# Six of twelve shifts of a grouped convolution as plain fp32 products on 32- and 64-column tiles, and the first mixing in fp32

## The reference

```
x = x + L0(x); x = x + L1(x); x = x + L2(x); x = x + L3(x)

L0, L2:  att   = softmax(mlp(cond) @ W2 + b2)            # (128 samples, 8)
         agg_w = einsum('bk,koi->boi', att, weight)      # a 128 x 128 matrix for each sample
         out   = einsum('boi,bih->boh', agg_w, x) + (att @ bias_k)[:, :, None]
L1, L3:  out   = conv1d(x, weight, 9 taps, padding 4, 4 groups of 32 channels)
                 + (cond @ c_weight.T)[:, :, None] + bias[None, :, None]
```

## Time and profile before

| | |
|---|---|
| median of 3 runs | 2906.19 us (2905.75 to 2907.77) |
| profiled execution: its own time, its span | 2907.99 us, 2905.7 us |
| PE, PEld busy | 2882.7 us (99%), 2860.9 us (98%) |
| DVE, ACT, POOL busy | 2420.1 us (83%), 1668.6 us (57%), 1482.6 us (51%) |
| instructions of PE | 49240 matmuls, as many loads |
| granted clock, mean over the span | 0.997 |

### The profile page before, as it was taken

How to read it: one execution, slowest core, us unless ns; L and a number is a source line. 1 busy time by engine, 2 the same in 40 slices (tenths; PEclk the granted TensorE clock), 3 DMA queues, 4 the chain that set the end, 5 groups by cost and what they waited for, 6 DMA issues and landing times.

```text
span 2905.7 us, 122950 instructions
## 1 busy us (share of the span) xinstructions
PE 2882.7 (99%) x49240; PEld 2860.9 (98%) x49240; DVE 2420.1 (83%) x2589; ACT 1668.6 (57%) x2593; POOL 1482.6 (51%) x1546
## 2 busy tenths in 40 slices
PE   8999999999999999999999999999999999999998
PEld 7999999999999999999999999999999999999998
DVE  8888888888888888888888888888888888888884
ACT  5555555555555555556565656565556555655564
POOL 3445554555455545544554455445544554455452
PEclk9999999999999999999999999999999999999999
DMA  6777777777777777777777777777777777777774
GB/s 160 198 199 201 202 196 203 198 202 196 202 197 202 198 202 196 204 196 204 193 204 197 204 193 206 198 203 194 204 199 203 197 200 200 202 203 193 201 202 138
DMA packets 374536, 573.17 MB, mean 197 GB/s; under 512 B 63336, under 2 KB 226800, under 8 KB 358128
## 3 DMA queue, kind: packets, MB, share of 16 engines
q1 hardware_dynamic: 325744, 506.17, 63.8%
q10 hardware_dynamic: 48768, 66.65, 9.1%
HBM read 271.63 MB, written 167.77 MB: 151 GB/s over the span
## 4 chain that ended last, share of the span: by engine, by line
PE 98%; DVE 1%; ACT 0%; DMA 0%; issue 0%; ACTq 0%; SPq 0%
PE ps L354 74%; PE ps L339 24%; ACT x_t L530 0%; DVE prod L592 0%; DVE y L635 0%; DVE m_sum L595 0%; PE ps L267 0%; PE ps L262 0%; DMA mixed<-m_own 0%; DVE m_own L603 0%; DMA m_parts<-mixed 0%; DVE m_own L601 0%; DVE xp L627 0%; DVE conv_parts L567 0%; ACT L449 0%
## 5 line engine op out<-in xcount | busy, mean ns | idle before, releaser
L354 PE MATMUL ps<-y,conv_parts 32*128 32x512 f32 x36864 | 2735.2, 390 | 2.2 <-DVE y L635 2.2
L354 PEld LDWEIGHTS ps<-y,conv_parts 32*128 32x128 f32 x36864 | 2533.4, 184 | 17.5 <-issue 2.3
L500 ACT ACTIVATE y<-ps,bias 128x512 fp32r<-128x512 f32 x1536 | 1045.4, 690 | 748.6 <-PE ps L354 710.6
L635 DVE SCALAR_TENSOR_TENSOR y<-ps,bias,y 128x512 fp32r<-128x512 f32 x1536 | 1074.4, 747 | 417.4 <-ACT y L500 415.0
L703 POOL COPY bias<-bias_table 128x4 f32 (+3 forms) x512 | 99.1, 209 | 1383.3 <-DMA o_ch<-o_ph 1344.5
L709 POOL TENSOR_TENSOR xp<-x_t,xp 128x512 fp32r<-128x512 f32 x508 | 787.4, 1581 | 3.9 <-ACT xp L469 3.9
L339 PE MATMUL ps<-xp,m_parts 32*128 32x512 f32 x6144 | 653.2, 391 | 7.5 <-DVE y L635 3.7
L339 PE MATMUL ps<-y,m_parts 32*128 32x512 f32 x6144 | 652.4, 390 | 0.0
L716 POOL COPY o_t<-o_ch 128x512 f32<-128x512 f32 x508 | 630.1, 1358 | 8.4 <-DMA o_ch<-o_ph 8.4
L533 ACT ACTIVATE o_ph<-ps,bias 128x512 f32<-128x512 f32 x508 | 330.5, 686 | 435.6 <-PE ps L354 431.1
L339 PEld LDWEIGHTS ps<-xp,m_parts 32*128 32x128 f32 x6144 | 557.9, 184 | 10.3 <-issue 4.1
(11 more groups left out here) (53 smaller groups left out, 53.3 us busy)
## 6 DMA issues: line engine op xcount, KB each, us to landing
x_t<-x SPq DMA_DIRECT2D x512, 256.0 KB, 5.6
m_parts<-mixed SPq DMA_DIRECT2D x1020, 128.0 KB, 3.7
out<-o_t SPq DMA_DIRECT2D x127, 1024.0 KB, 4.0
o_ch<-o_ph SPq DMA_DIRECT2D x1016, 64.0 KB, 2.0
o_ch<-o_ph ACTq DMA_DIRECT2D x1016, 64.0 KB, 3.7
mixed<-m_own SPq DMA_DIRECT2D x256, 128.0 KB, 2.1
conv_raw<-conv_w SPq DMA_DIRECT2D x2, 768.0 KB, 11.8
mix_sb<-mix_w SPq DMA_DIRECT2D x2, 576.0 KB, 9.1
```

The costliest lines, as they stand in the source:

```text
L354: ins = nc.tensor.matmul(ps[:, 4 + t, :], conv_parts[layer][rows, w, PH * q + p_in, :], src[rows, a, p_in, q:q + N], start=(k == 0), stop= ...
L500: nc.scalar.activation(dst, src, ACT.Identity, bias=bias[layer][:, k % WIDTH[layer]:k % WIDTH[layer] + 1]).then_inc(high_set[layer], 1)
L635: nc.vector.scalar_tensor_tensor(out=dst, in0=src, scalar=bias[layer][:, k % WIDTH[layer]:k % WIDTH[layer] + 1], in1=high.bitcast(fp32), o ...
```

## The change

- **Convolutions.** Shifts 3 to 8 (`DENSE`) stay as they were: three passes, row tiles of 32 by 128, 18 rounds for each convolution. Shifts 0, 1, 2, 9, 10, 11 (`SPARSE`) run as plain fp32 products, one per piece, on those column blocks alone that are not zero: 8 pieces of 64 or 32 columns per group, so 32 products per convolution, in three product-rounds. In a product-round the pieces of a group cover the four column blocks and the four groups the four row blocks. The moving operand is an unsplit fp32 copy (`y1_full`, `y3_full`), the stationary one `conv_raw`. Convolution 3 runs sparse first, then dense; convolution 1 dense first, then sparse.
- **First mixing.** One plain fp32 product of 128 by 128 by 512 for each quarter of x, from `x_t` and `m_sum[0]` as they are. The cast of x, POOL's subtraction, the split of the matrix, its store and its four loads for layer 0 go away, and x comes in one transfer.
- **Evictions.** ACT writes the full copy and HIGH for y1 and y3 (two instructions for one); DVE's LOW of these is now a subtraction of two SBUF tiles and no longer reads PSUM. y2 is as before.
- **No stagger.** The four tiles of a layer run round by round.
- **Queues.** All 16 transfers o_ch<-o_ph are issued by SP.
- **Tail.** The last sample's o_ph is regrouped by 16 small fp32 products on PE and copied in order to x_t by ACT and DVE, 64 lanes each; before, sixteen instructions of 32 lanes did it.

```diff
+    DENSE = range(PH - 1, SHIFTS - PH + 1)
+    SPARSE = (((10, 2, 2), (0, 0, 1), (9, 1, 1)),
+              ((1, 0, 2), (2, 2, 1), (11, 3, 1)),
+              ((2, 0, 2), (9, 2, 2)))
...
         y1 = sb("y1", [128, 2, PH, HALO], f32r)
+        y1_full = sb("y1_full", [128, PH, HALO])
...
         y3 = sb("y3", [128, 2, PH, HALO], f32r)
+        y3_full = sb("y3_full", [128, PH, HALO])
...
             def load_x(j):
+                sp.dma_start(flat(x_t, "q n"), x[j]).then_inc(x_in, 16)
...
+            def first_mix(i, inner):
+                pe.wait_ge(summed[0], i + 1)
+                pe.wait_ge(x_in, 16 * (i + 1))
+                if not inner and i == 0:
+                    pe.wait_ge(mix_b_read, 2)
+                if not inner and i == 1:
+                    pe.wait_ge(ctx_read, 2)
+                for q in range(G):
+                    if inner or i >= 2:
+                        pe.wait_ge(high_set[2], nth(i - 2, q))
+                    nc.tensor.matmul(ps[:, q, :], m_sum[0][:], x_t[:, q, :], start=True, stop=True).then_inc(mm[0], 1)
+            def second_mix(i, inner):
+                pe.wait_ge(m_in, 16 * G * i)
+                for g in range(G):
+                    pe.wait_ge(low_set[1], nth(i - 1, g))
+                    for n, (m, a) in enumerate(PASSES):
+                        first, final = g == 0 and n == 0, g == G - 1 and n == len(PASSES) - 1
+                        for p in range(PH):
+                            rows = slice(CG * p, CG * (p + 1))
+                            if first and has(i, inner, 0):
+                                pe.wait_ge(high_set[0], nth(i, p))
+                            elif first:
+                                pe.wait_ge(high_set[2], nth(i - 2, p))
+                            ins = nc.tensor.matmul(ps[:, p, :], m_parts[rows, g, m, :], y2[rows, a, g, :], start=first, stop=final)
+                            if final:
+                                ins.then_inc(mm[2], 1)
+            def sparse(layer, src, begins, wait_bank):
+                for r, units in enumerate(SPARSE):
+                    for t in range(G):
+                        rows = slice(CG * t, CG * (t + 1))
+                        if r == 0 and begins:
+                            wait_bank(t)
+                        for s, p, width in units:
+                            q, p_in = divmod(s, PH)
+                            final = r == len(SPARSE) - 1 and not begins
+                            ins = nc.tensor.matmul(ps[CG * p:CG * (p + width), 4 + t, :],
+                                                   conv_raw[layer][rows, 128 * s + CG * p:128 * s + CG * (p + width)],
+                                                   src[rows, p_in, q:q + N], start=(r == 0 and begins), stop=final)
+                            if final:
+                                ins.then_inc(mm[1], 1)
+            def dense(layer, src, begins, wait_bank):
+                order = sorted(DENSE, key=lambda s: (s % PH, s))
+                for k, s in enumerate(order):
+                    q, p_in = divmod(s, PH)
+                    for n, (w, a) in enumerate(PASSES):
+                        first = k == 0 and n == 0 and begins
+                        final = k == len(order) - 1 and n == len(PASSES) - 1 and not begins
+                        for t in range(G):
+                            rows = slice(CG * t, CG * (t + 1))
+                            if first:
+                                wait_bank(t)
+                            ins = nc.tensor.matmul(ps[:, 4 + t, :], conv_parts[layer][rows, w, s - DENSE[0], :],
+                                                   src[rows, a, p_in, q:q + N], start=first, stop=final)
+                            if final:
+                                ins.then_inc(mm[3], 1)
+            def step(i, inner):
+                now, last, before = has(i, inner, 0), has(i, inner, 1), has(i, inner, 2)
+                def free3(t):
+                    if last:
+                        pe.wait_ge(low_set[1], nth(i - 1, t))
...
+                def free1(t):
+                    if before:
+                        pe.wait_ge(phases_set, nth(i - 2, t))
                     elif last:
...
+                        pe.wait_ge(low_set[1], nth(i - 1, t))
...
+                if now:
+                    first_mix(i, inner)
+                if not inner and i == 0:
+                    att_to_all(1)
+                if before:
+                    if not inner and i == 2:
                         pe.wait_ge(conv_set, 2)
...
+                    pe.wait_ge(high_set[2], 4 * (i - 1))
+                    sparse(3, y3_full, True, free3)
+                    pe.wait_ge(low_set[2], 4 * (i - 1))
+                    dense(3, y3, False, free3)
+                if last:
+                    second_mix(i, inner)
+                if now:
+                    if not inner and i == 0:
+                        pe.wait_ge(zeros_set, 1)
+                        pe.wait_ge(conv_set, 1)
+                    pe.wait_ge(low_set[0], 4 * (i + 1))
+                    dense(1, y1, True, free1)
+                    if not inner and i == 0:
+                        side_bias()
+                        pe.wait_ge(full_first, G)
+                    sparse(1, y1_full, False, free1)
+            def last_regroup():
+                pe.wait_ge(phases_set, 4 * B)
+                for p in range(PH):
+                    for g in range(G):
+                        rows = slice(CG * p, CG * (p + 1))
+                        nc.tensor.matmul(ps[CG * g:CG * (g + 1), p, :], consts_sb[rows, CG * p:CG * (p + 1)], o_ph[rows, g, :],
+                                         start=True, stop=True).then_inc(regroup_mm, 1)
...
+            def high(layer, j, k, src, dst, full=None):
+                act.wait_ge(mm[layer], 8 * j + 2 * (k + 1) if layer == 1 else nth(j, k))
                 if k == 0:
                     act.wait_ge(bias_set[layer], j + 1)
...
+                column = bias[layer][:, k % WIDTH[layer]:k % WIDTH[layer] + 1]
+                if full is not None:
+                    nc.scalar.activation(full, src, ACT.Identity, bias=column)
+                nc.scalar.activation(dst, src, ACT.Identity, bias=column).then_inc(high_set[layer], 1)
+            def full_of_first():
+                for q in range(G):
+                    act.wait_ge(low_set[0], q + 1)
+                    nc.scalar.activation(segment(y1_full, q), by_phase(q), ACT.Identity, bias=bias[0][:, 0:1]).then_inc(full_first, 1)
...
+                elif now:
+                    act.wait_ge(mm[1], 8 * i)
+                    for q in range(G):
+                        high(0, i, q, by_phase(q), segment(y1[:, HIGH], q), segment(y1_full, q))
...
+                        nc.scalar.activation(o_ph[:, g, :], ps[:, 4 + g, :], ACT.Identity,
+                                             bias=bias[3][:, g:g + 1]).then_inc(phases_set, 1)
+                    if final:
+                        act.wait_ge(regroup_mm, G * PH)
+                        act.wait_ge(mm[0], 4 * B)
+                        for q in range(G):
...
                 if last:
+                    if inner or i > 1:
+                        act.wait_ge(mm[3], 4 * (i - 1))
...
-                        high(2, i - 1, p, y3[:, HIGH, p, 1:N + 1], ps[:, p, :], not inner and i == 1)
...
+            def low(layer, j, k, dst, full, high):
+                dve.wait_ge(high_set[layer], nth(j, k))
+                nc.vector.tensor_tensor(dst, full, high.bitcast(fp32), ALU.subtract).then_inc(low_set[layer], 1)
...
+                elif now:
+                    if inner or i + 1 < B:
+                        matrix(0, i + 1)
+                    for q in range(G):
+                        low(0, i, q, segment(y1[:, LOW], q), segment(y1_full, q), segment(y1[:, HIGH], q))
+                    matrix(2, i)
+                    halves(i)
...
+                        low(2, i - 1, p, y3[:, LOW, p, 1:N + 1], y3_full[:, p, 1:N + 1], y3[:, HIGH, p, 1:N + 1])
...
```

More of the change, by code:

```diff
@@ L168, in by_phase, with last_in_time, segment, conv_dense @@
             return ps[:, q, :].rearrange("c (m p) -> c p m", p=PH)
-        def last_out(g, p):
-            return flat(x_t, "g n")[CG * g:CG * (g + 1), :].rearrange("c (n p) -> c p n", p=PH)[:, p, :]
-        def segment(part, q):
-            return y1[:, part, :, 1 + q * (N // PH):1 + (q + 1) * (N // PH)]
+        def last_in_time(q, half):
+            rows, part = slice(64 * half, 64 * half + 64), slice(q * N // PH, (q + 1) * N // PH)
+            return x_t[rows, q, :].rearrange("c (n p) -> c n p", p=PH), ps[rows, 0:PH, part].rearrange("c p n -> c n p")
+        def segment(tile, q):
+            return tile[:, :, 1 + q * (N // PH):1 + (q + 1) * (N // PH)]
+        def conv_dense(layer):
+            return conv_raw[layer][:, DENSE[0] * 128:(DENSE[-1] + 1) * 128]
         block = ctx.enter_context(nc.Block())
@@ L297, in _ @@
```

(58 more changed lines are left out.)

324 lines of the change are left out of this document (87 added, 237 removed).

## The result

The changed kernel takes 9525.72 us (median of 4 runs, 9524.56 to 9530.17), the kernel before 2905.97 us (4 runs, 2905.33 to 2907.77): a ratio of 3.278, 95% interval 3.272 to 3.284. The forecast was 2749 us. It was wrong by a factor of 3.5, and in the direction.

What follows compares the result with a forecast made beforehand. PE, busy 99% of the span, was taken as the bound. Its terms summed to 21.10 us per sample instead of 22.31, -155 us over 128 samples; with -2 us for edges, 2905.7 became 2749 us, range 2640 to 2920.

Steps and rivals of the forecast that it cites:

- 2.58 us per convolution if all tiles of a product-round run side by side: Sparse shifts on PE: three product-rounds of two 0.43 us records, lower bound 2.58 us; 2.75 taken, upper bound 2.88.
- Rival 2: Sparse parts: each turn between 64 and 32 columns empties the array; 17.9 us per convolution, 6630 us in all; chance 0.08.
- the sum: PE time per sample, convolutions, mixings, shape changes and waits added: 21.10 us instead of 22.31; this case had 0.73.
- Two records of 0.43 us per product: Plain fp32 products on PE: 512 columns take two records of 0.43 us, 0.86 us; mixing 0's four take 3.44.
- Sparse parts: Six sparse shifts of each convolution as fp32 products on PE: 2.75 us per convolution, 5.50 us per sample.
- Changes of shape: Around mixing 0 and between sparse and dense: four per sample at 0.2 us, 0.8 us (0.4 if loads hide).
- Dense rounds and mixing 2: Parts left unchanged on PE, per sample: 36 dense rounds 8.37 us, 12 rounds of mixing 2 2.79 us.
- the waits: PE stalls for evictions at the start of convolutions 3 and 1: 0.2 us per sample counted for both.
- Evictions without stagger: After convolution 1, ACT and DVE need 3.8 us; mixing 0 with its shape changes covers 3.8; stall 0 to 0.2.
- Rival 3: Evictions on ACT and DVE become the bound; LOW of y2 1.2 us later cancels the gain, 2906 us; chance 0.08.
- Edges: Start, first steps, last convolution 3 and tail of the span: gains and new waits net about -2 us.
- Rival 1: Sparse parts: an fp32 product's record pair holds PE's queue; 14.2 us per convolution, 5680 us in all; chance 0.11.

Runs made afterwards that it cites:

- e1: Changed kernel with the same 32 sparse products per convolution sorted by width, each product-round having one width: 2762.03 us, 0.951 of the kernel before.
- e3: Changed kernel with the 64-column pieces of all four groups ahead of the 32-column ones in mixed product-rounds, 5 stretches instead of 17: 3293.76 us.
- e5: Changed kernel with only convolution 3 sorted by width, convolution 1 still alternating between 64 and 32 columns: 6190.04 us.
- e2: Changed kernel with every 64-column piece cut into two of 32, 48 products per convolution, convolution 3 dense first: 2849.19 us, 0.981 of the kernel before.
- e6: e1 with mixing 0 as twelve fp32r products in three passes instead of plain fp32: 2753.66 us, 0.946 of the kernel before.

## Why the prediction was wrong

**The step that failed** is "2.58 us per convolution if all tiles of a product-round run side by side", from which 2.75 was taken. The condition doesn't hold when neighbours differ in width. Rival 2 described it, down to the turn: 16 groups of one product or two, each with its own two records and a turn, 17.9 us per part. Measured: 27.9 and 28.1 us per part. At full clock it would be 16.8, by the stretches ahead of the fall of the clock (a turn costs 0.12 to 0.14 there, where the prediction took 0.2 from the earlier trace rows). e1 and e3 show that the turns are the cause: the products are the same, and time follows the number of stretches. I had given this 0.08, on the ground that the changes in the earlier trace rows were between the whole array and a part of it. That was no evidence against: each change of shape that the trace had did cost 0.2, and none was free. The price at stake (a factor of two in the whole kernel) stood beside it, and the one row that looked alike pointed to it.

The Trainium skill, "TensorEngine Tiling (Array Packing)", section "Key Properties", says that a change of tiling mode drains TensorE. By that rule rival 2 was the forecast; the traces agree, with 0.81 to 0.84 us of held loads at each turn in e1 and e3 against 0.20 to 0.25 within one width.

**The term that was missing** is the clock. Rival 2 came to 51.4 us per sample, the kernel takes 74.1. At full clock it would be 2 x 16.8 + 3.63 + 8.70 + 2.81 = 48.7; the other 25.4 us are the clock, at 0.50 for most of each part and for some microseconds behind. The prologue showed a dip (0.83 in two stretches), which I put in no rival; but there PE had just stood still for 2.9 and 3.7 us, and no row showed the clock falling under a busy PE. e5 shows that one alternating part suffices.

**Point by point, of the sum**, which e1 tests, since it does what the sum assumed but for one turn inside each part (2762.03 us, for 2749 forecast):
- *Two records of 0.43 us per product*: right. In e1 the loads of mixing 0 come every 0.43 us, eight records in 3.63 us with the change of shape behind them (forecast 3.44 + 0.2).
- *Sparse parts*: forecast 2.75 and 0.2 for the change of shape behind each, 2.95; measured 3.03, with one turn of about 0.24 inside that the forecast didn't have. Without that turn it would be 2.8, so the rest was forecast 0.16 too long. With 96 records (e2) it is 3.34.
- *Changes of shape*: forecast 0.2 each. Bare records come to 8.37 + 2.79 + 8 x 0.43 + 12 x 0.43 = 19.76 us, so 1.44 of the 21.20 are changes, and e1 has six, two of them inside the parts: 0.24 each. By the loads, mixing 0 has 0.2 beyond its records, a stretch of 16 products 0.21 to 0.27, one of four or eight 0.15 to 0.18 (e3), one of one or two 0.12 to 0.14: it grows with the products in it. Dense rounds and mixing 2 are 8.70 and 2.81. With one change of shape the dense rounds were forecast at 8.57, mixing 2 at 2.79, and the waits, which e1 doesn't show, at 0.2. The total, 21.20 us, answers to 21.10 forecast; that it is this close is in part luck: the two turns inside the parts, which the forecast didn't have, stand against waits that didn't come and records that took less.
- *Evictions without stagger*: forecast 3.8 us of path against 3.8 of cover. In e1 line 609 ends 3.5 us after the end of convolution 1, and the cover is 3.63. In e6 it is 2.99, and 0.47 us stand open. The path was forecast 0.3 and the cover 0.2 too long; that they are equal to within 0.15 us was right. Rival 3 is the next bound, not this one.
- *Edges*: forecast -2 us. In e1 the span less 128 x 21.20 is 46.3 us, for 50.0 before: -3.7. The last convolution 3 waits 4.8 us for ACT, where 5.5 were forecast.
- *Rival 1, the pair of records holds the queue*: refuted. 16 first records are in flight together in e1, before any second one; in e3 four products take 1.01 us and eight 1.04, where the rival's 0.43 for each would give 5 x 0.43 = 2.15 and 9 x 0.43 = 3.87. The Trainium skill, "TensorE: Matmul & The Clock Gate", section "The mechanism" of Part 3, has matmuls start in the program's order. Stretch by stretch they do, by the loads shown above; but a second record doesn't hold back the next tile's first one, as I had read it, and the traces don't say where in the program a single record stands.

What stays open: why a change of width empties the array was not looked into, only that it does. What else than the number of products on the array brings the clock down was not varied. Whether turns between 128 columns and 64 are of the same kind was seen only at the parts' ends. And why e2's loads come slower in the second and third product-round, which goes with its 0.31 us, is not explained.

## What to carry to other kernels

Before small tiles are packed side by side, write down the sequence of tile shapes in the order of the program and count the stretches, not the products: here a stretch cost its records and 0.12 to 0.27 us more, however few tiles it filled, so pieces go sorted by shape. Where a rival costs a factor and the nearest row speaks for it, it gets more than a small chance, and an experiment that sorts the order is cheap. A busy PE tells nothing of the array: look at the loads' idle time on "issue" and at the granted clock.

## What the runs showed of the hardware

- The granted clock fell to half while PE was recorded busy without a gap, when the stretches held one or two small products (0.50 from 4036 to 4060 us), and came back during dense rounds, at about 4062. With four and more in a stretch it was 0.997 (e3).
- The two records of an fp32 product don't stand behind each other in the queue of all tiles: the first records of all 16 tiles run together, then the second ones (e1, 16 records in flight in a window of 0.15 us).
- A stretch takes 1.01 to 1.04 us at full clock for 4 or 8 products on tiles of their own, and 0.98 to 1.00 for one or two.
- On DVE the subtraction of line 615 took 911 ns in e1, 689 in the changed kernel (line 616), the same operation. In e1 POOL's line 691 went from 1114 to 1470 ns as well. That they disturb each other is what this suggests; no run separates them.
